# 32 unused bytes before and after the feed-forward weights in SBUF

## The reference

```python
x = x + attn_a(layernorm(x), ...)   # SSM with rotation: scan over the 512 tokens, 8 heads
x = x + ffn(layernorm(x), w1, ...)
x = x + attn_b(layernorm(x), ...)   # delta rule: scan over the 512 tokens, 8 heads of 32
x = x + ffn(layernorm(x), w1, ...)  # the same weights again

def ffn(x, w1, s1, w2, s2, h1, ..., h2, ..., w3, ...):   # tlin(x, w, s) = (x @ w.T) * s
    h = silu(tlin(x, w1, s1)) * tlin(x, w2, s2)          # 256 -> 1024
    h = gelu(tlin(h, h1, ...))                           # 1024 -> 1024
    h = gelu(tlin(h, h2, ...))                           # 1024 -> 1024
    return tlin(h, w3, ...)                              # 1024 -> 256
```

## Time and profile before

| | |
|---|---|
| median of 3 runs | 2565.39 us (2564.84 to 2567.19) |
| the profiled execution | 2566.16 us, its span 2564.4 us |
| TensorE matmuls, busy | 2281.9 us, 89% of the span |
| TensorE weight loads, busy | 2034.3 us, 79% |
| VectorE, ScalarE, GpSimd, busy | 1363.8, 1118.9, 841.3 us |
| mean granted clock of TensorE | 0.965 of the full clock |

### The profile page before, as it was taken

One profiled execution on the slowest core, in us unless ns is written; L12 is line 12 of the kernel. 1 busy time (PEld: TensorE's weight loads), 2 busy tenths in 40 slices (PEclk: granted clock), 3 DMA queues, 4 the chain that ended last, 5 costly groups with the idle time before them and its releaser, 6 DMA issues.

```text
span 2564.4 us, 61597 instructions
## 1 busy us (share of the span) xinstructions
PE 2281.9 (89%) x25057; PEld 2034.3 (79%) x25088; DVE 1363.8 (53%) x3348; ACT 1118.9 (44%) x2160; POOL 841.3 (33%) x1003
## 2 busy tenths in 40 slices
PE   4679998887899988998999989999889999899888
PEld 3558887776888878887888878888788887897788
DVE  4565374465636555466644657356563655445531
ACT  3346332552335733365334743357333663333323
POOL 3123333323333333332323333342333333233233
PEclk8789999988999999999999999999999999999999
DMA  7000000000000001000010000100010000000000
GB/s 251 1 1 1 1 18 19 1 1 5 27 22 1 1 19 31 6 1 3 18 32 4 1 3 18 35 2 1 9 40 7 1 1 18 24 4 18 17 11 9
DMA packets 85468, 43.84 MB, mean 17 GB/s; under 512 B 69936, under 2 KB 80048, under 8 KB 85168
## 3 DMA queue, kind: packets, MB, share of 16 engines
q1 hardware_dynamic: 81504, 28.11, 4.4%
q0 software_dynamic: 3664, 11.53, 1.4%
HBM read 27.05 MB, written 12.58 MB: 15 GB/s over the span
## 4 chain that ended last, share of the span: by engine, by line
PE 61%; DVE 22%; issue 7%; POOL 5%; ACT 2%; DMA 2%; DVEq 0%; SPq 0%; POOLq 0%; ACTq 0%
PE F L1277 29%; PE Q L1336 5%; DVE ti L1127 4%; PE F L1257 4%; DVE prod L1125 3%; PE Q L1407 3%; PE F L1299 2%; PE Q L1393 2%; POOL hA_lo L586 2%; DVE hid L937 2%; PE Q L1370 2%; PE Q L1434 2%; POOL rn L638 2%; PE Q L1502 2%; PE Q L1348 1%
## 5 line engine op out<-in xcount | busy, mean ns | idle before, releaser
L586 POOL TENSOR_TENSOR hA_lo<-hid,hA_hi 128x256 fp32r<-128x256 f32 (+1 forms) x384 | 357.9, 934 | 723.8 <-ACT hA_hi L715 414.7
L1277 PE MATMUL F<-hA_hi,h_sb 128*128 128x256 f32 x2048 | 514.7, 291 | 8.6 <-DVEq L940 4.3
L1277 PE MATMUL F<-hB_hi,h_sb 128*128 128x256 f32 x2048 | 510.5, 289 | 2.1 <-POOL hB_lo L586 1.5
L1277 PE MATMUL F<-hA_lo,h_sb 128*128 128x256 f32 x2048 | 498.3, 283 | 0.0
L1277 PE MATMUL F<-hB_lo,h_sb 128*128 128x256 f32 x2048 | 496.0, 282 | 0.0
L1277 PEld LDWEIGHTS F<-hA_hi,h_sb 128*128 128x128 f32 x2048 | 392.4, 192 | 20.3 <-DVEq L940 5.7
L1277 PEld LDWEIGHTS F<-hB_hi,h_sb 128*128 128x128 f32 x2048 | 390.9, 191 | 12.8 <-POOL hB_lo L586 4.3
L1277 PEld LDWEIGHTS F<-hA_lo,h_sb 128*128 128x128 f32 x2048 | 393.3, 192 | 1.7 <-issue 1.4
L1277 PEld LDWEIGHTS F<-hB_lo,h_sb 128*128 128x128 f32 x2048 | 391.6, 191 | 0.5 <-issue 0.5
L1257 PE MATMUL F<-xf_hi,w_sb 128*128 128x256 f32 x1024 | 282.9, 310 | 81.2 <-DVEq L940 59.4
L711 ACT ACTIVATE hid<-F,sh_sb 128x256 f32<-128x256 f32 x256 | 121.3, 474 | 407.3 <-PE F L1277 405.5
(11 more groups left out here) (196 smaller groups left out, 4146.6 us busy)
## 6 DMA issues: line engine op xcount, KB each, us to landing
h_sb<-h_dram POOLq DMA_DIRECT2D x2, 4096.0 KB, 24.2
x_sb<-x_dram SPq DMA_DIRECT2D x8, 512.0 KB, 4.4
a_scr<-amv SPq DMA_DIRECT2D x32, 128.0 KB, 2.3
au<-a_scr SPq DMA_DIRECT2D x8, 512.0 KB, 3.2
t_scr<-ti SPq DMA_DIRECT2D x8, 512.0 KB, 2.6
tbd<-t_scr SPq DMA_DIRECT2D x128, 32.0 KB, 2.0
out_dram<-x_sb SPq DMA_DIRECT2D x8, 512.0 KB, 3.0
w_sb<-w_dram POOLq DMA_DIRECT2D x3, 1024.0 KB, 9.0
```

The source lines that it names most:

```text
L586: pool.tensor_tensor(lo, hid[:, n % 2, 0:w, :], hi.bitcast(F32), ALU.subtract).then_inc(f_lo.handle, 1)
L1277: last = pe.matmul(ps[:, i * TOK:(i + 1) * TOK], w[:, k, o:o + P], part[:, k, :], start=(i == 0 and k == 0 and part is src[0]), stop=(i == ...
```

## The change

Two tiles of eight fp32 numbers (32 bytes of each partition) are declared, one in front of w1_sb and one behind w3_sb. No instruction reads or writes them.

```diff
@@ -174,11 +174,13 @@
             return ctx.enter_context(nc.semaphore(name))
 
 
+        line_pad = sb("line_pad", [P, 8])
         w1_sb = sb("w1_sb", [P, 2, HID], F32R)
         w2_sb = sb("w2_sb", [P, 2, HID], F32R)
         h1_sb = sb("h1_sb", [P, KT, HID], F32R)
         h2_sb = sb("h2_sb", [P, KT, HID], F32R)
         w3_sb = sb("w3_sb", [P, KT, D], F32R)
+        line_pad2 = sb("line_pad2", [P, 8])
         win_sb = sb("win_sb", [P, 2, W_IN])
         wout_sb = sb("wout_sb", [P, 4, D])
         wqkvb_sb = sb("wqkvb_sb", [P, 2, W_QKVB])
```

## The result

The changed kernel takes 2548.78 us (median of 4 runs, 2545.82 to 2551.29), the kernel before beside it 2566.29 us (4 runs, 2564.84 to 2569.73). The ratio is 0.9929, 95% interval 0.9912 to 0.9947: 17.5 us or 0.7% faster. The forecast was no change, 2566 us, and the range's low end of 2554 us misses the result by 5 us.

What follows compares the result with a forecast made beforehand. TensorE was taken as the bound, its feed-forward matmuls starting every 120 ns. The terms 0 + 0 + 0.4 + 0 + 0 = +0.4 us on 2566.2 us gave 2566 us, no change, with a range from 2554 to 2600.

Steps and rivals of the forecast that it cites:

- so the two sweep past each other through all relative positions within a line whatever their start: Feed-forward matmuls: the stream is read twice as fast as the weights, so an offset merely moves when they meet; 0 us.
- Inside these bounds I take 0: The 10,240 half-line-off loads beside streaming matmuls: taken as 0, with bounds up to 41 us slower or as much faster.
- an eighth and a sixteenth of a loss for one line more: Bounds for touching one more line: 0.5 ns for a load (9 lines for 8), 0.6 ns for w3's stream (17 for 16).
- the loads cost the running matmul 4 ns, and some 9 ns are there without them: Split of the 13 ns lost per feed-forward matmul at full clock, from durations of 283 ns with a load, 279 without.
- Contention vanishes (faster): Rival at the feed-forward matmuls: half a line's distance ends load-stream collisions, 120 to 116 ns, -27 to -41 us; chance 0.12.
- a part of it: Smaller faster case at the feed-forward matmuls: one step of 0.83 ns gained, -6 to -8 us, 2557 to 2560; chance 0.10.
- forecast share of 66%: Share of a change in feed-forward matmul pace let through to the end: 898 of 1352 us lie on the chain.
- Contention doubles: Slower rival at the feed-forward matmuls: loads collide twice as often with the stream, 124 ns, 2592 to 2615 us; chance 0.13.
- one line more costs a step: Slower rival at the feed-forward matmuls: one or two clock steps (0.83 or 1.7 ns) on 10,240, 2571 to 2583 us; chance 0.18.
- +0.4 us: w3 streamed from half a line off at L1299: 0.6 ns on 1,024 matmuls, 0.6 us in all, 0.4 us through.

Runs made afterwards that it cites:

- d1: Kernel before with 96 unused bytes added behind w3_sb, weights left in place; 2563.0 us in one run, beside 2568.0.
- c2: Kernel before with each matmul at L1277 streaming one word 256 times, so it computes other numbers; 2538.31 us in one run, beside 2569.26.
- d3: Kernel before with 256 unused bytes added behind w3_sb, weights left in place; 2572.6 us in one run, beside 2569.3.
- a2: Kernel before with one 32-byte tile in front of w1_sb and none behind w3_sb, so everything moves together; 2568.55 us, ratio 0.9996.
- b4: Kernel before with 64 unused bytes added behind w3_sb, weights left in place; 2545.5 us in one run, beside 2568.6.
- e1: Kernel before with 128 unused bytes between h2_sb and w3_sb and 64 behind w3_sb; 2542.8 us, ratio 0.9893.
- d4: Kernel before with 192 unused bytes added behind w3_sb, weights left in place; 2550.2 us in one run, beside 2568.0.
- a3: Kernel before with 32-byte tiles in front of xf_hi and behind hB_lo, moving the feed-forward activations and no weights; 2547.35 us, ratio 0.9906.
- b1: Kernel before with each weight tile 64 bytes longer and the weights beginning 8 bytes into it; 2565.05 us in one run, beside 2568.58.
- a4: Changed kernel with the second tile in front of w3_sb, not behind, so w3_sb keeps its place; 2550.25 us, ratio 0.9920 to the kernel before.
- a1: Kernel before with one 64-byte tile in front of w1_sb and none behind w3_sb, so everything moves together; 2569.04 us, ratio 0.9992.
- b3: Kernel before with each weight tile 64 bytes longer and the weights beginning 48 bytes into it; 2554.93 us in one run, beside 2568.58.
- c1: Kernel before with each load at L1277 reading one word 128 times, so it computes other numbers; 2545.86 us in one run, beside 2569.26.

## Why the prediction was wrong

**The step that failed** is "so the two sweep past each other through all relative positions within a line whatever their start", on which "Inside these bounds I take 0" rested. Whatever positions the two pass through, the start counts: a distance of +32 bytes modulo 256 takes 2.85 ns from the step at L1277, -64 takes 5.6, +96 nothing (d1). In c2 all that the stream's reads add measures 8.2 ns. And the unit was wrong: the argument went by lines of 64 bytes, and its bounds by an eighth and a sixteenth of a loss for one line more. No run shows such a line or such a share; the runs show a period of 256 bytes (d3), and being 32 bytes behind a multiple of 64 is of no importance by itself (a2, b4).

**The split "the loads cost the running matmul 4 ns, and some 9 ns are there without them"** was wrong too. It made 4 ns the most that a place could give, and e1's 5.6 ns pass that. It read durations of pipelined matmuls, 283 against 279 ns, as if they were steps. By the runs 5.0 ns (111.7 less 106.7) are the load's own pace (c2, with the earlier trace rows), at least 5.6 are the meeting (d4, e1), and the last 2.6 are undivided; so the part that is there without loads is at most 2.6 ns and not 9. The duration of one matmul without a load beside it says little of the pace of many.

**The rival that came true** is "Contention vanishes (faster)", and its reason, load and matmul of the earlier trace rows that start together at the same place, is what a2, a3 and c2 bear out. It had a chance of 0.12, and "a part of it" 0.10. Its size was off by the step: "120 to 116 ns" was 120 to 117.05, and at L1299 to 118.2. With 30.6 us in place of 41 saved, the forecast share of 66% gives 20 us, and 57% was measured. The result of 2549 lies between its two cases (2524 to 2538, and 2557 to 2560): the range took in the small one, one step of 0.83 ns, and the gain was 2.85 ns.

**"Contention doubles" and "one line more costs a step"** fell: none of the three lines of after got slower. That a new distance can also cost is seen elsewhere: b1's L1299 at 121.4 ns.

**w3, "+0.4 us".** L1301 did not get slower by the 0.6 ns of the sum; it got 1.6 ns quicker, which is 1.6 us of steps in all. With w3_sb in its old place (a4) it is back at 119.8, so the cause there is the same pair of operands.

**What held.** A new place for loads alone costs nothing and gains nothing (and a2 for loads beside a stream). Later tiles, DMAs and the work on VectorE, ScalarE and GpSimd count for nothing (a1; the profile's busy row). The Trainium skill's page "TensorE: Matmul & The Clock Gate" (Part 2, step 1) has the load take nothing from the running matmul; e1's 114.3 ns against 119.9, the same instructions with nothing but places changed, contradicts it for these float32r matmuls. By the Trainium skill's page "SBUF — State Buffer" (Specifications), with its line of 16 bytes, 32 bytes would be whole lines; the 2.85 ns that they gave, and the period of 256 bytes of d3, do not follow from that.

**What stays open.** Why a distance has the levels that it has, and what sets a stretch on one of them: +32 gives 116.7 and 117.8 ns, +64 and -64 give 113.3 and 117.8 in different shares, -32 118.2, -96 118.0, -56 121.4 and +96 nothing. A picture fits a part of it: the stream reads 1024 bytes in the time of the load's 512, so it gains 256 bytes on the load in about half a step, and two that start together meet three times in a step (at its start, middle and end), two that start apart twice; 8.2 / 3 = 2.7 ns a meeting gives 117.2 ns with two. It does not give the 113.3 of -64 nor the 120.0 of +96, so it is argued and no more. Of distances below 32 bytes one alone is clean, -16 at L1299 in b3; a matmul in another type was not tried.

## What to carry to other kernels

Where matmuls stream 4-byte words back to back with a weight load beside each, the place in SBUF of the loaded tile against the streamed one, modulo 256 bytes, can be worth some ns of each; here a stream that starts 64 bytes below the load took 5 of 120, and unused tiles of 128 and 64 bytes were all it needed. Try both directions, since +64 and -64 differ, and judge by the distance between starts in long runs without a wait: durations of pipelined matmuls and loads (188 ns in d1, at 120.0 ns a step) mislead. Here 44 to 57% of the saved steps arrived as time; look at the granted clock, over several runs, before a remainder is put down to the change.

## What the runs showed of the hardware

- The pace of a matmul with a weight load beside it depends on where the two read: 119.9 ns a step with both starting at the same place modulo 256 bytes, 114.1 to 118.7 at most other distances, 120.0 at +96, 121.4 at -56, 111.7 with the stream held on one word.
- The step goes in stretches at levels of its own (after: 116.7 and 117.8 ns; b4 and d4: 113.3 and 117.8, in opposite shares; c1: 113.4, 116.7, 120), so a mean of all starts is needed, and one window of a timeline can show either level.
- A load lasts 188 ns in place of 192 in after, and so does one in d1, whose step is 120.0; and c2, where the stream stands on one word, keeps 192 and is the quickest. The duration of a load doesn't tell the pace.
